# A vision-transformer layer on one core: the last three chunks of the patch embedding, taken by halves of the tokens

## The reference, cut to what matters

```python
def patch_embedding(x, gamma, beta, w, b):          # x: (8, 3, 128, 128)
    xc = concatenate((x, right, left, down, up), axis=1)      # five shifts, 15 channels
    tokens = patches_16x16(xc)                                 # (8, 64, 3840)
    normed = (tokens - mean(tokens)) * rsqrt(var(tokens) + 1e-5) * gamma + beta
    return normed @ w + b                                      # (8, 64, 192)

h = patch_embedding(x, ...)
h = h + attention(layernorm(h))    # 12 heads of 16, strided causal mask
h = h + experts(layernorm(h))      # 8 experts, 192 -> 768 -> 192, best two of 8 per token
```

## Time and profile before

| | |
|---|---|
| median of 3 runs | 188.11 us (187.97 to 188.87) |
| the profiled execution, its own time | 188.18 us |
| its span, first to last instruction | 186.4 us |
| PE busy | 174.7 us, 94% of the span |
| DVE, ACT, POOL busy | 139.3, 115.4, 83.0 us |
| granted TensorE clock, mean | 1.000 |

### The profile page before, as it was taken

The page is one execution under the profiler, slowest core; times in us unless marked ns, Lnnn a source line. Parts: engine busy times, 40 slices in busy tenths (PEclk is TensorE's granted clock), DMA queues, the critical chain, the costliest instruction groups (busy, mean ns, idle before and its releaser), DMA issues.

```text
span 186.4 us, 3467 instructions
## 1 busy us (share of the span) xinstructions
PE 174.7 (94%) x1137; PEld 148.8 (80%) x1137; DVE 139.3 (75%) x313; ACT 115.4 (62%) x206; POOL 83.0 (45%) x109
## 2 busy tenths in 40 slices
PE   5898999969989879899999999999999999999994
PEld 2485868949767658689899899899899899999994
DVE  5389987598457984897778788688688688787553
ACT  2489553734624364856786787777776875973730
POOL 7877601131698423930552652652652652560000
PEclk9999999999999999999999999999999999999999
DMA  5999999400104930037004504505505400000002
GB/s 122 260 284 256 223 223 271 108 0 2 43 23 148 261 82 0 0 93 207 0 0 143 153 0 125 170 2 144 151 0 157 139 2 0 0 4 0 0 0 84
DMA packets 14979, 18.08 MB, mean 97 GB/s; under 512 B 2467, under 2 KB 10776, under 8 KB 14966
## 3 DMA queue, kind: packets, MB, share of 16 engines
q1 hardware_dynamic: 14422, 17.90, 36.7%
q10 hardware_dynamic: 544, 0.03, 0.2%
HBM read 17.14 MB, written 0.39 MB: 94 GB/s over the span
## 4 chain that ended last, share of the span: by engine, by line
PE 62%; DVE 5%; POOL 3%; issue 2%; POOLq 0%; DVEq 0%
PE ps L369 29%; PE ps L1171 17%; PE ps L1173 8%; PE ps L1221 1%; PE ps L1220 1%; PE ps L1219 1%; DVE merge L1252 1%; PE ps L381 1%; DVE big_r L1252 1%; POOL h L577 1%; POOL halo L585 1%; DVE bn L1420 1%; PE ps L376 1%; POOL halo L590 1%; DVE shifted L1252 1%
## 5 line engine op out<-in xcount | busy, mean ns | idle before, releaser
L369 PE MATMUL ps<-big_r,wsplit 128*128 128x512 f32 (+1 forms) x245 | 61.5, 387 | 0.0
L777 ACT ACTIVATE early<-ps,b1t 128x512 f32<-128x512 f32 x48 | 32.8, 684 | 29.1 <-PE ps L369 27.4
L1171 PE MATMUL ps<-wsplit,big_r 128*128 128x384 f32 x168 | 49.7, 355 | 0.7 <-DVE big_r L1252 0.7
L1252 DVE TENSOR_TENSOR big_r<-early,big_r 128x512 fp32r<-128x512 f32 x48 | 35.9, 751 | 15.8 <-ACT big_r L332 15.3
L369 PEld LDWEIGHTS ps<-big_r,wsplit 128*128 128x128 f32 x245 | 41.9, 189 | 6.3
L1173 PE MATMUL ps<-wsplit,big_r 128*128 128x192 f32 x168 | 42.1, 250 | 0.0
L1171 PEld LDWEIGHTS ps<-wsplit,big_r 128*128 128x128 f32 x168 | 31.5, 188 | 2.7 <-issue 1.1
L1173 PEld LDWEIGHTS ps<-wsplit,big_r 128*128 128x128 f32 x168 | 32.0, 190 | 1.3
L332 ACT ACTIVATE big_r<-early 128x512 fp32r<-128x512 f32 x48 | 30.4, 632 | 1.5
L1592 DVE SCALAR_TENSOR_TENSOR merge<-sq,gates,merge 128x192 f32<-128x192 f32 x32 | 26.9, 864 | 0.0
L314 POOL TENSOR_TENSOR wsplit<-stage,wsplit 128x768 fp32r<-128x768 f32 x4 | 7.4, 1846 | 19.3 <-ACT wsplit L332 15.7
(11 more groups left out here) (242 smaller groups left out, 283.7 us busy)
## 6 DMA issues: line engine op xcount, KB each, us to landing
stage<-in_L_ffn_w SPq DMA_DIRECT2D x4, 576.0 KB, 6.8
early<-in_L_ffn_w SPq DMA_DIRECT2D x4, 576.0 KB, 6.0
shifted<-in_L_tok_w SPq DMA_DIRECT2D x6, 288.0 KB, 8.6
early<-in_x SPq DMA_DIRECT2D x6, 256.0 KB, 5.3
stage<-in_L_ffn_w SPq DMA_DIRECT2D x4, 384.0 KB, 3.9
stage<-in_L_ffn_w SPq DMA_DIRECT2D x8, 192.0 KB, 4.9
early<-in_L_ffn_w SPq DMA_DIRECT2D x4, 384.0 KB, 3.1
early<-in_L_ffn_w SPq DMA_DIRECT2D x8, 192.0 KB, 4.4
```

The source lines that it names most:

```text
L369: mm = nc.tensor.matmul(dst, lhs, rhs, start=(first and n == 0), stop=(last and n == 4))
L777: nc.scalar.activation(gf[:, j % NG], ps[:, HPB[j % 4], :], ACT.Gelu, bias=b1t[:, bass.ds(k, 1)]).then_inc(s_gelu, 1)
L1171: nc.tensor.matmul(ps[:, AB[t], 0:2 * D], g_hi[:, j % NG, tok], w2c, start=(f == 0), stop=False)
L1252: return nc.vector.tensor_tensor(o, a, b, op)
```

## The change

Chunks 6, 7 and 5 are taken for tiles 0 and 1 first and then for tiles 2 and 3, with the bias rows and mean squares where they were among the first half. So that everything for chunk 5 is there when its first half comes, DVE does the last two merges ahead of the halo's low weights, and chunk 5's low weights ahead of the mask reductions. On ACT `small_high(2)` goes ahead of the `beta_part` copy, and the last two parts of expert 0's weights (`split_high(0, 2)`, `(0, 3)`) go behind `high_parts(0)`. The six matmuls that nobody reads are taken out; the two behind the masks stay (their count now has a name). Every other line is as it was.

```diff
--- before.py
+++ after.py
@@ -261,6 +261,7 @@
         PTB, PVB, ATB, OB, N2B = (2, 4), (0, 7), (1, 6), (2, 4), (3, 5)
         RB, VBB, RTB = 7, 3, 6
         EARLY = 3
+        IDLE = 2
         LAG = 3
         HPB = [0, 1, 2, 3]
         AB = [4, 5, 6, 7]
@@ -684,9 +685,9 @@
             merged_high(1, 2)
             small_high(0)
             small_high(1)
+            small_high(2)
             act.wait_ge(s_beta, 1)
             copy(beta_part, ps[:, BETAB, 0:D]).then_inc(s_betapart, 1)
-            small_high(2)
             act.wait_ge(s_beta, 2)
             copy(u_bias[:], ps[:, BETAB, 0:2 * D].rearrange("p (k n) -> p k n", k=2)).then_inc(s_bias, 1)
             nc.scalar.activation(st4[:, 1], ps[:, BETAB, 400:400 + 2 * TT:2], ACT.Copy,
@@ -698,8 +699,6 @@
             split_high(0, 1)
             small_high(3)
             copy(b1t[:], ps[:, WB[3], 400:400 + E * FC]).then_inc(s_wathi, 1)
-            split_high(0, 2)
-            split_high(0, 3)
 
             def high_parts(g, ps_ready, banks, dst, done):
                 act.wait_ge(ps_ready, g + 1)
@@ -741,6 +740,8 @@
 
             last_columns_again(0, 0, n1)
             high_parts(0, s_nt, NTB, nt, s_nhi)
+            split_high(0, 2)
+            split_high(0, 3)
             act.wait_ge(d_bqk, 16 * BQK_DMAS)
             transposed_q(0)
             last_columns_again(0, 1, n1)
@@ -898,9 +899,9 @@
             beta_products(0)
             beta_products(1, (0, 1))
 
-            def whole_chunk(ch):
+            def chunk(ch, tiles=range(TT)):
                 pe.wait_ge(s_wlo, ORDER.index(ch) + 1 - (ORDER.index(ch) > 5))
-                for t in range(TT):
+                for t in tiles:
                     mm = embed(ch, t)
                     if ch == ORDER[-1] and t % 2:
                         mm.then_inc(s_emb, 1)
@@ -909,12 +910,12 @@
             pe.wait_ge(s_mw, 1)
             pe.wait_ge(s_xhi, 4)
             pe.wait_ge(s_xlo, 4)
-            whole_chunk(0)
-            whole_chunk(1)
+            chunk(0)
+            chunk(1)
             beta_products(1, (2, 3, 4))
             pe.wait_ge(s_xhi, XGROUPS)
             pe.wait_ge(s_xlo, XGROUPS)
-            whole_chunk(2)
+            chunk(2)
 
             pe.wait_ge(s_m, 1)
             pe.wait_ge(s_xsq, XGROUPS)
@@ -929,8 +930,8 @@
                     mm = nc.tensor.matmul(ps[tile, SQB, :], ones_f[0:HALO, 0:32], sq_halo[0:HALO, n - 2 * C],
                                           start=False, stop=True)
             mm.then_inc(s_sumsq, 1)
-            whole_chunk(3)
-            whole_chunk(4)
+            chunk(3)
+            chunk(4)
 
             pe.wait_ge(s_wdup, 2)
             small_transposes(0)
@@ -947,8 +948,8 @@
             pe.wait_ge(s_hhi, 1)
             pe.wait_ge(s_hlo, 1)
             pe.wait_ge(s_mw, 2)
-            whole_chunk(2 * C)
-            whole_chunk(2 * C + 1)
+            chunk(2 * C, (0, 1))
+            chunk(2 * C + 1, (0, 1))
             pe.wait_ge(s_first, 1)
             pe.wait_ge(s_betapart, 1)
             for k in range(2):
@@ -958,7 +959,10 @@
                 mm = nc.tensor.matmul(ps[:, BETAB, 400 + 2 * t:402 + 2 * t], sq_part[:, t * P:(t + 1) * P],
                                       first_rows[:, 0:1].broadcast_to([P, 2]), start=True, stop=True)
             mm.then_inc(s_beta, 1)
-            whole_chunk(2 * C - 1)
+            chunk(2 * C - 1, (0, 1))
+            chunk(2 * C, (2, 3))
+            chunk(2 * C + 1, (2, 3))
+            chunk(2 * C - 1, (2, 3))
             pe.wait_ge(s_watlo, 1)
             small_transposes(3)
 
@@ -1085,11 +1089,9 @@
             pe.wait_ge(s_watlo, 2)
             pe.wait_ge(s_bias, 1)
             pe.wait_ge(s_watlo, 3)
-            for _ in range(6):
-                nc.tensor.matmul(ps[:, SB[0], :], xh[:, 0, 0:P], xh[:, 0, :], start=True, stop=True)
             masks(0)
             masks(1)
-            for _ in range(2):
+            for _ in range(IDLE):
                 nc.tensor.matmul(ps[:, NTB[0], :], xh[:, 0, 0:P], xh[:, 0, :], start=True, stop=True)
             transposes(0, n1, s_n, lambda t: t + 1, NTB, s_nt, s_ndup)
 
@@ -1362,13 +1364,13 @@
             dve.wait_ge(s_hhi, 1)
             tt(xl[0:HALO, 2 * C:NX], x_halo[0:HALO], xh[0:HALO, 2 * C:NX].bitcast(F32),
                ALU.subtract).then_inc(s_hlo, 1)
-            low_weights(6, slice(2 * C, NX), wm_halo[0:HALO], slice(0, HALO))
             merge(1, 2, 3)
             merge(1, 2, 4)
+            low_weights(6, slice(2 * C, NX), wm_halo[0:HALO], slice(0, HALO))
+            low_weights(7, C + 2, w_sum[:, 1, 2], slice(0, P))
             dve.wait_ge(c_mask, E)
             nc.vector.tensor_reduce(mask[:, 0:NK], tri_p[:], AX_X, ALU.add).then_inc(s_mask, 1)
             nc.vector.tensor_reduce(mask[:, NK:], near[:], AX_X, ALU.min).then_inc(s_mask, 1)
-            low_weights(7, C + 2, w_sum[:, 1, 2], slice(0, P))
 
 
             def small_low_parts(groups):
```

## The result

The changed kernel takes 186.91 us (median of 19 executions, 186.23 to 187.82) against 188.11 us for the kernel before in the same runs: a ratio of 0.9942, interval 0.993 to 0.9955. The forecast was 187.0, within 186.5 to 188.2. The profiled execution has a span of 185.1 us where it was 186.4.

What follows compares the result with a forecast made beforehand. Bound: a chain from PE's embedding through DVE, POOL and attention to PE's experts. 188.18 less 1.15 for four embeds gave 187.03, all else nothing; 186.96 against the median, called 187.0, range 186.5 to 188.2 us.

Steps and rivals of the forecast that it cites:

- The path: PE's embedding until DVE's start at 34.63 us, then DVE, POOL and attention, then experts on PE; everything behind that start shifts.
- the first rival, the gain taken up: Behind 36 us, waits or moved ACT work absorb half or all the gain: 187.5 to 188.2 us; chance 0.18.
- Four embeds, 1.15 us: On PE, four embeds instead of eight ahead of the bias rows start DVE's group 0 1.15 us earlier, at 33.48.
- Nothing for the moves on DVE and ACT: Reordered merges, low weights, copies and expert-weight parts cost nothing, at most 0.1 us on ACT; cover before `transposed_q(0)` 0.7 us.
- DVE's idle ahead of its start: Sign that the forecast is right: DVE idles about 1.7 us before starting group 0 near 33.5 us.
- The second half is not waited for: Tiles 2 and 3 finish on PE at 35.0 us; DVE comes to group 1 at about 36.9, without waiting.
- Nothing for the fillers: Removing six unread PE matmuls at 35.77 to 37.26 us gains nothing; PE idles 1.0 us instead of 0.71.
- The slower rival: PE's clock falls between 37.2 and 48 us, adding 3.9 us to the path: 190.9 us; chance 0.08.
- the slack of 0.8 us: Group 1's low part on DVE could have started at 46.6 us but did at 47.42: 0.8 us of slack.

Runs made afterwards that it cites:

- halves_only: The kernel before with only chunks 6, 7 and 5 embedded by halves on PE; old DVE and ACT orders, six fillers kept: 186.59 us, ratio 0.992.
- rest_only: The changed kernel with chunks 6, 7 and 5 whole again, keeping the DVE and ACT reordering and the missing six fillers: 188.46 us, ratio 1.0044.
- six_back: The changed kernel with the six unread matmuls put back in front of the masks: 186.76 us, ratio 0.9926.
- six_out: The kernel before with its six unread matmuls taken out and nothing else changed: 189.45 us, ratio 1.0065.
- no_fillers: The changed kernel without the last two unread matmuls behind the masks as well: 187.27 us, ratio 0.9964.
- half234_beta: The changed kernel with chunks 2, 3, 4 also by halves, beta products and copy earlier, masks behind group 0's transposes, no fillers: 185.21 us, ratio 0.9846.

## Why the prediction was right, point by point

**The path.** That everything behind DVE's start moves with it is shown best by one difference, the span less the time of DVE's start. It is 186.4 - 34.63 = 151.8 us before, 185.1 - 33.29 = 151.8 after, and 151.7 to 151.9 in the other seven kernels whose profiled execution kept the clock (mean 0.998 or more), for starts from 31.87 to 34.35. Nothing between 36 and 77 us took any of it up, so the first rival, the gain taken up, is out.

**Four embeds, 1.15 us.** The distance from chunk 3's first embed to DVE's start was 34.63 - 25.45 = 9.18 us before and is 33.29 - 25.27 = 8.02 after: 1.16. `halves_only` has 8.02 as well (33.08 - 25.06) and `rest_only` 9.18 (33.99 - 24.81). The term and its cause are shown.

**Nothing for the moves on DVE and ACT.** Shown by `halves_only`, and by `six_back`, which differs from it in these moves alone. They could have been left out. The moved parts of `split_high` left a cover of 0.88 us ahead of `transposed_q(0)`, where the prediction had 0.7:

```profile
41.63 0.47 ACT L712 ACTIVATE sq<-ps,bqk 128x256 f32<-128x256 f32 x1 [0.88 <-PE ps L370]
```

**DVE's idle ahead of its start.** This sign was forecast wrong: 1.7 us, and it was 2.82. I had taken 1.15 from the 2.89 before and forgotten that the moves also fill DVE's own holes of 0.84 and 0.21 us, so that DVE is done earlier with what comes before. 1.74 and 1.05 make 2.79. Nothing hangs on it, since DVE waits for PE there in any case: for 2.12 us even in `halves_only`, which has the old orders.

**The second half is not waited for.** Shown; DVE came to it 1.9 us after PE had it ready (36.73 against 34.8).

**Nothing for the fillers.** This step was wrong, though it did not spoil the total. I read the clock off one execution, where it stays up in all slices and also in the emptiest stretch, and took that for a property of the kernel. It differs from execution to execution: the kernel before falls to the lower clock for a while in 17 of 55, the changed one in 8 of 19. Holding the clock is what the fillers do here. In the changed kernel their loss costs 0.15 us of median (186.91 against 186.76 with the six back), too little to be told apart from nothing by these intervals; with the halves the gap they leave is only 0.94 us. In the kernel before, where DVE comes later, the same edit costs 0.65% of the time (`six_out`).

**The slower rival** had the mechanism and its place right, and its price and chance wrong: I gave it 0.08, and a fall came in 8 of 19 executions but cost little. I let the clock be low until all transposes of group 1 were through, 4.7 us of delay on PE, 3.9 on the path. The runs show 0.6 us for one fall (187.35 against 186.78) and 1.4 us for the long one (188.21 against 186.79). Even in the long one PE was at full clock again shortly after 45 us, so it ended that work later by 2.3 us, not 4.7, counted from the transposes of group 0 (46.84 - 37.96 = 8.88 against 44.63 - 38.07 = 6.56); less the slack of 0.8 us this makes 1.5. The span less DVE's start says the same: 153.4 us in the profiled executions of `no_fillers` and `six_out`, which are at 0.982, and 152.3 in that of `rest_only`, at 0.991, for the 151.8 of those that kept the clock. A fall to 0.991 thus halves the gain of the change. A long one would take up all of it; none of the 19 executions of the changed kernel had one. In the kernel with whole chunks the missing fillers did make a loss (`rest_only`, `six_out`). The Trainium skill, "TensorE: Matmul & The Clock Gate", Part 1, says that activity holds the clock up; by that rule the missing fillers speak against the change. These runs agree: with the six fillers back the clock fell in 0 of 6 executions, without them in 8 of 19.

**That the number came out so close is partly luck.** The halves are worth 1.16 us in the traces, and the medians differ by 1.20. Both medians include executions in which the clock fell, and these raise both by about the same: the changed kernel's by 0.13 us (186.91 against 186.78 for the executions that kept the clock), that of the kernel before by 0.11 to 0.17 us in the three sets whose clocks are on record (187.84 against 187.73, 187.94 against 187.80, 187.89 against 187.72). So a cost that I had put at nothing nearly cancels in the difference. Within one set, between executions that kept the clock, the halves alone take off 187.72 - 186.59 = 1.13 us. The 187.75 - 186.78 = 0.97 that the table gives for the whole change compares different sets.

## What to carry to other kernels

When one engine produces for several consumers in groups, put all that the first group needs ahead of anything that only the second needs: the producer does the same work and the chain behind it starts earlier by what was taken from in front, here 0.29 us for each embed, until another operand or the second group becomes the limit. Check two things in the profile: that the second group still arrives before the consumer comes to it, and that the producer finds its inputs at the earlier time. Matmuls whose results nobody reads may be doing a job; before taking them out look at the granted clock of many executions, not of one.

## What the runs showed of the hardware

I had not expected the granted clock to differ from one execution of the same kernel to the next. The mean over the span took only the values 1.00, 0.991 and 0.982 (within 0.002), and longer idle of PE ahead of the normalised tokens (at 37 to 39 us) went, by and large, with more of the lower ones: 0 of 24 executions with no idle there, 1 of 11 with 0.27 us, 0 of 5 with 0.37, 17 of 55 with 0.71, 8 of 19 with 0.94, 9 of 12 with 1.41, and 22 of 22 with 2.11 (`six_out` and `rest_only`). Another idle of 0.78 us follows in all of these. In `half234_beta`, where the masks fill that second idle, it was 0 of 5 with 0.80 us; five executions are too few to say that this is why. The idle times are each from one profile, and the counts are of this kernel's stretch alone. In the three profiled executions in which the clock fell (`rest_only`, `no_fillers`, `six_out`) it was back at the full level by 46 us, while PE was busy without a gap.
